# Two edits of a decoder layer kernel: the first read's normalised rows on ScalarE with its products ahead of its turning, and the output units in token tile order

## The reference, cut to what matters

```
x = x + attn(_layernorm(x), ...)             # 32 heads, 4-bit weights
x = x + xattn(_layernorm(x), ctx_1024, ...)  # rat_read, attention, rat_write, rat_read, mlp, rat_write
x = x + ffn(_layernorm(x), ...)              # one 1024x1024 product with weights from a lookup table

def _layernorm(x, eps=1e-05):
    return (x - mean(x)) / sqrt(var(x) + eps)

def rat_read(res, W, gamma, beta, n):        # res: the normalised rows
    y = einsum('blhc,hoc->bloh', res.reshape(b, l, 256, 4), W)
    yn = (y - y.mean(-1)) * rsqrt(y.var(-1) + eps)
    return yn * gamma + beta

# ffn: the mask that chooses the 8-bit weights compares a row's norm with 64, all rows here are below it;
y = x @ w_l.T + bias                         # w_l: (1024, 1024), 4-bit codes through a table per row
```

## Time and profile before

| what | before |
|---|---|
| median of 3 runs | 1828.83 us |
| the profiled execution's own time | 1830.57 us |
| its span | 1828.9 us |
| TensorE busy, matmuls / weight loads | 1602.4 us (88%) / 1062.5 us (58%) |
| VectorE / ScalarE / GpSimd busy | 1357.6 (74%) / 912.7 (50%) / 577.6 us (32%) |
| first read | about 1159.6 to 1254.8 us, 95 us |
| last stage up to the end | about 1628 to 1828.9 us, 201 us |

### The profile page before, as it was taken

The page is one execution under the profiler, slowest core; times in us unless marked ns, Lnnn a source line. Parts: engine busy times, 40 slices in busy tenths (PEclk is TensorE's granted clock), DMA queues, the critical chain, the costliest instruction groups (busy, mean ns, idle before and its releaser), DMA issues. The chain is left out here.

```text
span 1828.9 us, 21013 instructions
## 1 busy us (share of the span) xinstructions
PE 1602.4 (88%) x6880; PEld 1062.5 (58%) x6880; DVE 1357.6 (74%) x2078; ACT 912.7 (50%) x1682; POOL 577.6 (32%) x463
## 2 busy tenths in 40 slices
PE   4799999999999999999999898667999657888799
PEld 3466666666666666666666665465555336445444
DVE  7788888887788788788788775773677588568961
ACT  3354454555554544544555443234368666557620
POOL 2346445455455454554554443102110100000000
PEclk9999999999999999999999999677989755899899
DMA  4001111111111110110100100412443200010111
GB/s 179 23 24 58 35 37 45 35 47 35 35 47 35 35 58 24 50 43 24 58 24 24 47 12 23 169 47 50 101 84 45 89 1 0 1 35 12 47 63 40
DMA packets 30963, 84.20 MB, mean 46 GB/s; under 512 B 6006, under 2 KB 7304, under 8 KB 30600
## 3 DMA queue, kind: packets, MB, share of 16 engines
q1 hardware_dynamic: 30856, 82.87, 15.3%
HBM read 70.27 MB, written 12.58 MB: 45 GB/s over the span
## 5 line engine op out<-in xcount | busy, mean ns | idle before, releaser
L518 DVE SCALAR_TENSOR_TENSOR acc<-pj,sc_o,acc 128x1024 f32<-128x1024 f32 x232 | 293.9, 1280 | 89.3 <-PE pj L649 86.0
L518 DVE SCALAR_TENSOR_TENSOR q_acc<-pj,sc_q,q_acc 128x1024 f32<-128x1024 f32 x224 | 286.5, 1279 | 34.0 <-PE pj L649 28.6
L628 POOL TENSOR_TENSOR prob<-prob,inv_total 128x512 f32<-128x512 f32 (+3 forms) x256 | 189.6, 745 | 385.2 <-DVE inv_total L560 385.2
L649 PE MATMUL pj<-ctx_hi,w_o 128*128 128x512 f32 x528 | 237.1, 449 | 25.6 <-ACT spare L407 12.2
L649 PE MATMUL pj<-zT_hi,w_q 128*128 128x512 f32 x512 | 224.9, 439 | 4.4 <-PEq L81 3.1
L649 PE MATMUL pj<-ctx_lo,w_o 128*128 128x512 f32 x528 | 207.8, 393 | 0.0
L461 ACT ACTIVATE prob<-ps,low_max 128x512 f32<-128x512 f32 (+3 forms) x256 | 134.2, 527 | 144.4 <-DVE low_max L553 144.3
L649 PE MATMUL pj<-zT_lo,w_q 128*128 128x512 f32 x512 | 203.3, 397 | 0.0
L703 PE MATMUL ps<-kT,qT 128*128 128x512 f32 (+3 forms) x512 | 186.7, 447 | 10.4 <-ACT prob L461 10.3
L727 PE MATMUL pv<-probT,v 128*128 128x512 f32 (+3 forms) x512 | 169.4, 433 | 0.0
L649 PEld LDWEIGHTS pj<-ctx_hi,w_o 128*128 128x128 f32 x528 | 99.0, 188 | 110.6 <-DVE acc L518 43.1
(11 more groups left out here) (330 smaller groups left out, 3104.2 us busy)
## 6 DMA issues: line engine op xcount, KB each, us to landing
raw_o<-in_w_o SPq DMA_DIRECT2D x33, 512.0 KB, 3.6
raw_q<-in_w_q SPq DMA_DIRECT2D x32, 512.0 KB, 3.6
x_ring<-qk_kept SPq DMA_DIRECT2D x64, 128.0 KB, 4.4
ln_x<-in_x SPq DMA_DIRECT2D x8, 512.0 KB, 7.4
raw_kv<-in_w_k SPq DMA_DIRECT2D x8, 512.0 KB, 3.5
raw_kv<-in_w_v SPq DMA_DIRECT2D x8, 512.0 KB, 4.5
x<-in_x SPq DMA_DIRECT2D x8, 512.0 KB, 7.0
x_kept<-x SPq DMA_DIRECT2D x8, 512.0 KB, 2.9
```

Source lines behind the costliest of these rows:

```text
L518: dve.scalar_tensor_tensor(out=dst, in0=pj[slot][:], scalar=scale, in1=dst, op0=ALU.mult, op1=ALU.add).then_inc(evac_v, 1)
L628: pool.tensor_tensor(prob[:, k % PROBS, 0:w], prob[:, k % PROBS, 0:w], inv_total[:, n:n + 1].to_broadcast([P, w]), ALU.mult).then_inc(norm ...
L649: ins = pe.matmul(pj[slot][:, b * S:(b + 1) * S], lhs, part[:, b * S:(b + 1) * S], start=n == 0, stop=n == 1)
```

## The change

The first read: VectorE's `finish(i)` forms a 128x1 tile shift = -mean * t in place of h; ScalarE has a new `normalise(i)`, which forms h = t * x1 + shift in one 128x1024 ACTIVATE and stands between Read.root(i-2) and copy_h(i-1); and on TensorE `products` stands ahead of `turn_y`. The last stage: units go by token tile, (tile 0, g 0), (tile 0, g 1), (tile 1, g 0) and so on; `turn_z(1)` no longer stands ahead of the first unit; both tables are new. ScalarE's list in the last stage is the same as before, and SyncE issues the same transfers, the stores in the new order of units.

```diff
@@ residual_read
-        sd, r, t = sb("r_sd", [P, NT]), sb("r_r", [P, NT]), sb("r_t", [P, NT])
+        sd, r, t, shift = (sb(f"r_{n}", [P, NT]) for n in ("sd", "r", "t", "shift"))
...
                 if 1 <= i <= NT:
                     pe.wait_ge(done, i)
                     rd.turn_h(pe, i - 1)
+                if 1 <= i <= NT:
+                    rd.products(pe, i - 1)
                 if i >= 2:
                     rd.turn_y(pe, i - 2)
-                if 1 <= i <= NT:
-                    rd.products(pe, i - 1)
...
+            def normalise(i):
+                act.wait_ge(shifted, i + 1)
+                act.activation(h[:, i, :], x1[:, i, :], ACT.Identity, bias=shift[:, i:i + 1],
+                               scale=t[:, i:i + 1]).then_inc(done, 1)
...
                 if 1 <= i <= NT:
+                    normalise(i - 1)
                     rd.copy_h(act, i - 1)
...
-                dve.tensor_scalar(h[:, i, :], x1[:, i, :], mv[:, i, 0:1], t[:, c],
-                                  ALU.subtract, ALU.mult).then_inc(done, 1)
+                dve.tensor_scalar(shift[:, c], mv[:, i, 0:1], -1.0, t[:, c], ALU.mult, ALU.mult).then_inc(shifted, 1)
...
@@ the tables
-TURN_AFTER = {0: 2, 1: 3, 3: 4, 5: 5, 6: 6, 7: 7}
-EVICT_AFTER = {4: (0, 1), 5: (2, 3), 6: (4, 5), 7: (6,)}
+TURN_AFTER = {0: 1, 2: 2, 3: 3, 5: 4, 7: 5, 9: 6, 11: 7}
+EVICT_AFTER = {3: (0,), 4: (1, 2), 5: (3, 4), 6: (5, 6), 7: (7,)}
...
@@ write_norm_forward
-        units = [(b * half + i, g) for b in range(B) for g in range(2) for i in range(half)]
+        units = [(i, g) for i in range(NT) for g in range(2)]
...
             turn_z(0)
-            turn_z(1)
-            for u in range(4 * half):
+            for u in range(2 * NT):
...
                 for u in EVICT_AFTER.get(i, ()):
-                    if u < half:
-                        add_bias(u)
+                    if u % 2 == 0:
+                        add_bias(u // 2)
                     evict(u)
             for u in range(sum(len(v) for v in EVICT_AFTER.values()), len(units)):
-                if 2 * half <= u < 3 * half:
-                    add_bias(units[u][0])
+                if u % 2 == 0:
+                    add_bias(u // 2)
                 evict(u)
```

More of the change, by code:

```diff
@@ L947, in residual_read @@
         loaded = [sem(f"r_loaded{i}") for i in range(NT)]
-        chain, turned, added, var_ready, sd_ready, done, moved = (sem(f"r_{n}") for n in (
-            "chain", "turned", "added", "var", "sd", "done", "moved"))
+        chain, turned, added, var_ready, sd_ready, shifted, done, moved = (sem(f"r_{n}") for n in (
+            "chain", "turned", "added", "var", "sdr", "shifted", "done", "moved"))
         made, shaped, angles_in, rw_in, consts_in, ready, trig = (sem(f"a_{n}") for n in (
```

## The result

The change makes the kernel **slower**: 1840.29 us median of 13 runs (1835.31 to 1844.26) against 1828.31 us of the kernel before (13 runs, 1826.78 to 1832.95). The ratio is 1.0057, with a 95% interval of 1.0048 to 1.0066, so 9 to 12 us. The forecast was no change, 1830.7, and the measurement lies 5.3 us above the upper end of its wider range, 1835.0. The profiled execution of the change is one of its longer runs, 1844.0 us, with a span of 1842.3, where that of before had 1830.57 and 1828.9. So the two traces are 13.4 us apart where the medians are 12.0 apart.

A forecast was written before the change was run, and what follows sets the result against it. No engine was full: a ring across engines bound the first read, TensorE's units the last stage. +6.0 and -4.1 made +1.9 us on 1828.83, so 1830.7 us, no change (chance 0.70); range 1827 to 1834, wider 1826.8 to 1835.0.

The forecast's parts named there:

- A stage in front of the other only shifts it: Costing rule: each edited stage is costed by itself; an earlier stage only moves a later one in time.
- The first read, +6.0: First read: seven intervals +4.9 us, first products +0.6, stage end +0.5; together +6.0 us, bounds +1.5 and +11.
- The ring: First read, per tile: products, turning yn, six copies, two roots, h, turning h; 10.13 to 11.01 us, 10.4 taken, before 10.08.
- The tail: End of first read: last root waits behind ScalarE's copies; +1.7 us at low clock, nothing at high, 0.5 taken.
- The last stage, -4.1: Last stage: first unit starts 2.9 us earlier, last unit ends at 1821.7 against 1825.7; -4.1 us, bounds -5.6 and -2.5.
- one gap: Last stage: TensorE idles once, 1.5 us ahead of the turn of tile 5, which waits for copy_z(4) on ScalarE.
- Rival 1: First read: low clock nearly throughout, ScalarE's copies delay the roots in every tile; +6.8 us in all, 1835.6 us, chance 0.21.
- Rival 2: First read: higher clock reaches the products, half the intervals at 8.0 us; total -6.3 us, 1822.5 us, chance 0.09.
- Rival 3: Last stage: VectorE's 11 us delay reaches TensorE at several turns, stage only -1; total +5, 1833.8 us, counted in Rival 1's chance.
- the 3.4 us that were weighed for it: First read: h on ScalarE at 1.24 against 0.81 us; as the only effect, 8 x 0.43 = 3.4 us more.

The follow-up runs named there:

- e1: Kernel before with only the read's edits (h on ScalarE, products ahead of turning), last stage as before: 1842.29 us, ratio 1.0068.
- e2: Kernel before with only the last stage's new unit order and two tables, first read as before: 1825.61 us, ratio 0.9982.
- e10: Kernel before with the new units and tables, soft_log(1) moved ahead of copy_z(1), exponents 4 and 5 ahead of copy_z(2): 1825.59 us, ratio 0.9972.
- e3: Kernel before with only h moved to ScalarE, TensorE's order as before: 1829.86 us, ratio 1.0005.
- e12: The change plus 48 transposes on TensorE that nobody reads, in the front of cross attention: 1841.06 us, ratio 1.0054 to the kernel before.

## Why the prediction was wrong

- **"A stage in front of the other only shifts it": the step that failed.** It priced cross attention, the stage of 171 us right behind the first edit, at nothing, unlooked at. It took 9.0 us more in the profiled pair, at a clock of 0.86 in place of 0.92. Of the 11.5 us by which that pair's span (1842.3) misses the forecast's 1830.8, 9.0 are there, 1.5 in the read and 1.2 in the last stage. On the medians, e1 costs 13 us with a read that is 6.4 longer in its trace, and the delays show a surplus of 5 us with the read's order as before. A later start alone made the stage longer, and the profile of before showed the material: the earlier trace rows has it change level inside the read, and the page gives cross attention a clock of 7 to 9 tenths.
- **The first read, +6.0: mechanism right, size +7.5.** The ring is the one described, in all its members, and seven intervals took 72.2 us where 72.1 stood. The first products came 0.6 us later within the stage, as forecast. The first interval was 10.0 and not 9.7. The tail was taken at +0.5 and was +1.9: the last root waited for the copies, and TensorE's products and turning ahead of these ran at the low clock throughout, which the text gave as its other end (+1.7). As the unchanged read took 95.2, 93.3 and 93.2 us in the traces of before, e2 and e10, the +7.5 is the figure of this pair.
- **The last stage, -4.1: mechanism right, size -3.0.** VectorE waited 4.9 us for root(3), 4.7 for exponent(4) on top of the lateness that came before it, and 3.5 for the store; one gap of 1.66 us where 1.5 stood. The first unit took 9.59 us and not 9.0 (the low level lasted 5.4 us into it, by the 2.7 us that it lost, and not 4.3 as before); the rest is tenths. The comparison of e2 confirms the 3 us. (The row of 55.10 us is 6.89 for each of its eight units, where the text has 6.87, the distance from start to start; this changes nothing.)
- **Rival 1** was on the right side for the wrong reason. It would have had intervals of 11.0; the six were 9.7 to 10.9 and 10.4 on average. Its 1835.6 is still 4.7 us short, for cross attention is at nothing in it too. **Rival 2** named the clock, but inside the read alone and as a gain; the read's mean granted clock fell from 0.66 to 0.60. **Rival 3**, that VectorE's 11 us of lateness would reach TensorE more than once, fell: one gap.
- The range (to 1835.0) was narrower than the read's and the last stage's own upper bounds together (+11 and -2.5, 1837.3), and even these hold nothing for a third stage.
- Moving h to ScalarE at 1.25 us in place of 0.81 costs nothing by itself that e3 could show. With the 3.4 us that were weighed for it, e3 would be at 1.0019, above its interval. The advice of the Trainium skill (ScalarE: Activation LUTs, Rules for kernel authors) to use VectorE for additions and multiplications agrees with the instruction's duration here and not with the kernel's time: ScalarE had slack.

What stays open: which event sets the moment at which the clock rises, why most executions of the change fall on the long side (three of 13 below 1837, eight above 1839.5), why the fillers do not help it, and how much of its median loss, beyond the read's 7.5 us, each later stage carries. The traces give one execution each, and e12 shows that one can mislead.

## What to carry to other kernels

When an edit lengthens or shortens a stage, the next stage that is bound by TensorE has to be read too: compare its granted clock in windows laid at equal distances from its first instruction, before calling the edit's cost its own length. Move an instruction behind a group on an in-order engine only together with what was moved to make that group late: h on ScalarE and products ahead of turning could each not be told from free, and cost 13 us together. Where a table moves one engine's turns, move the other engines' lists with it; here two moves in ScalarE's list gave another 1.6 us in the last stage of the trace (193.9 to 192.3), which the medians of e2 and e10 do not separate.

## What the runs showed that I had not expected

An idle stretch of 2.2 us at the end of one stage cost about 8 us (1.0044), with the rest of the program unchanged, and 48 transposes that compute nothing took 5.6 us off the kernel with a delay, and nothing off the change. The same 944 matmuls of cross attention took from 168 to 180 us. And a trace can be of an untypical execution: that of e3 is 5.5 us shorter than that of before, all of it in the read, while the medians of the two kernels cannot be told apart.
